# Two-layer GATv2 on one core: projection ahead of the scores, relus ahead of the weights, one set of waits a step

## What is computed

```python
xl = (x @ Wl + bl).reshape(n, HEADS, DIM)
xr = (x @ Wr + br).reshape(n, HEADS, DIM)
e = jax.nn.leaky_relu(xl[src] + xr[dst], NEG_SLOPE)
score = jnp.einsum('ehd,hd->eh', e, att)
smax = jax.ops.segment_max(score, dst, num_segments=n)
ex = jnp.exp(score - smax[dst])
denom = jax.ops.segment_sum(ex, dst, num_segments=n)
alpha = ex / (denom[dst] + 1e-16)
out = jax.ops.segment_sum(xl[src] * alpha[..., None], dst, num_segments=n)
```

## Time and profile before

| | us |
|---|---|
| median of 3 runs | 2266.37 |
| span of the profiled execution | 2743.9 |
| PE busy in it | 1964.3 (72%) |
| POOL busy | 1543.5 (56%) |
| ACT busy | 1411.6 (51%) |
| DVE busy | 1302.8 (47%) |
| DMA engines, mean over the span | 121 GB/s |

### The profile page before, as it was taken

One profiled execution on the slowest core, in us unless ns is written; L12 is line 12 of the kernel. 1 busy time (PEld: TensorE's weight loads), 2 busy tenths in 40 slices (PEclk: granted clock), 3 DMA queues, 4 the chain that ended last, 5 costly groups with the idle time before them and its releaser, 6 DMA issues. The chain is left out here.

```text
span 2743.9 us, 66371 instructions
## 1 busy us (share of the span) xinstructions
PE 1964.3 (72%) x19001; PEld 1307.1 (48%) x19001; DVE 1302.8 (47%) x5318; ACT 1411.6 (51%) x3474; POOL 1543.5 (56%) x1664
## 2 busy tenths in 40 slices
PE   4567777777777777777744777777777777777775
PEld 2234555554554555545533445544545545555453
DVE  7324554554544544544541344444444444444445
ACT  4324555555555555555542455555555555555554
POOL 4656666565566566565315666566556565565540
PEclk9778988989999998998966898999998999889997
DMA  5544444444454454444214444444444444444430
GB/s 133 166 111 127 127 130 128 132 130 128 130 131 128 129 132 129 128 133 128 73 56 117 122 125 128 126 121 129 128 125 128 123 125 127 125 124 128 124 107 7
DMA packets 236750, 332.67 MB, mean 121 GB/s; under 512 B 51011, under 2 KB 160491, under 8 KB 236395
## 3 DMA queue, kind: packets, MB, share of 16 engines
q0 software_dynamic: 75072, 208.30, 29.4%
q1 hardware_dynamic: 161322, 120.16, 14.9%
HBM read 308.02 MB, written 20.25 MB: 120 GB/s over the span
## 5 line engine op out<-in xcount | busy, mean ns | idle before, releaser
L982 POOL DMA_INDIRECT rows<-table,src_t x1564 | 1492.5, 954 | 995.5 <-PE psum L1182 367.9
L1428 DVE SCALAR_TENSOR_TENSOR acc<-acc,keep,psum 128x129 f32 x782 | 273.2, 349 | 1164.2 <-PE psum L1182 596.9
L1207 ACT COPY wgt<-psum 128x256 f32<-128x256 f32 x392 | 146.0, 373 | 1030.2 <-PE psum L1190 649.4
L1089 PE MATMUL psum<-lz,att_w 128*32 128x256 f32 x3128 | 281.2, 434 | 513.6 <-ACT lz L1200 444.6
L1103 PE MATMUL psum<-ident,rows 128*128 128x128 f32 x3128 | 578.4, 315 | 34.9 <-DMA rows<-table,src_t 34.9
L1103 PEld LDWEIGHTS psum<-ident,rows 128*128 128x128 f32 x3128 | 412.3, 160 | 237.5 <-issue 187.8
L1200 ACT ACTIVATE lz<-psum 128x512 f32<-128x512 f32 x782 | 427.8, 603 | 41.0 <-DMA table<-row 14.4
L1182 PE MATMUL psum<-rows,wgt 128*32 128x129 f32 x6256 | 313.8, 302 | 49.3 <-issue 45.9
L1089 PEld LDWEIGHTS psum<-lz,att_w 128*32 128x32 f32 x3128 | 64.4, 113 | 590.0 <-ACT lz L1200 509.4
L1106 PE MATMUL psum<-oh,xrw 96*128 96x256 bf16 x1564 | 344.4, 306 | 0.0
L1279 ACT ACTIVATE ex<-hold_s,peak 128x256 f32<-128x256 f32 x392 | 201.5, 514 | 138.4 <-issue 87.4
(11 more groups left out here) (257 smaller groups left out, 2100.1 us busy)
## 6 DMA issues: line engine op xcount, KB each, us to landing
xrw<-xr_split SPq DMA_DIRECT2D x782, 48.0 KB
relb<-rel_d SPq DMA_DIRECT2D x194, 192.0 KB
rows<-table,src_t POOLq DMA_INDIRECT x1564
relb<-cyc_d SPq DMA_DIRECT2D x194, 64.0 KB
xr_split<-split SPq DMA_DIRECT2D x50, 192.0 KB, 1.9
table<-row SPq DMA_DIRECT2D x50, 130.0 KB, 2.1
x_mid<-x SPq DMA_DIRECT2D x25, 64.0 KB
xo<-x_mid SPq DMA_DIRECT2D x25, 64.0 KB
```

The lines of the kernel that those rows point to most:

```text
L982: pool.indirect_dma_start(rows[:, ring(u), t, u % M, :, :].rearrange("p h c -> p (h c)"), None, s["tables"][layer][0:NP, :], bass.Indirect ...
L1089: m = pe.matmul(out[o:o + W, 0:UE], w["att_w"][:, h * W:h * W + W], lz[:, u % M, h * UE:h * UE + UE], start=False, stop=True, skip_group_c ...
L1428: m = v.scalar_tensor_tensor(a, a, s["keep"][:, u:u + 1], sum_bank(i - 6)[:, c:c + D + 1], ALU.mult, ALU.add)
```

## The change

- **PE order.** A step begins with the transposes of exp of step i-4, which stood at its end. Then come node stages 5, 13 and 9, then `project(i)` for both units, then `score(i-1)`, then the sums of step i-5 and the node work. Within the node work the combining matmuls (L1143) go from the end to the front.
- **PE waits.** `project` takes a whole step. Rows are counted by one semaphore for each of ten ring places, ranges by one for each of four. It waits once for rows and bank ahead of the first transpose, and once for range and one-hots ahead of the first one-hot matmul.
- **Masks.** The mask matmul of a unit, 64 columns wide, becomes two of 32 columns.
- **ACT order.** The relus of step i (before: of step i-1) come after the first node work, then the weights of step i-4 (before: i-5), the other node work, exp of step i-3 (before: i-4), then the scores of step i-1 (before: i-2), then `lin` of step i, which no longer waits for rows itself.
- **Buffers.** `lz`, the relus' output, gets four places, not two.
- **DVE.** `lowest` takes step i-2, not i-3, in the same place.

The diff, without the moved blocks that are the same on both sides:

```diff
-    rows_in = [sem(f"rows_in{i}") for i in range(ROWS)]
-    xr_in = [sem(f"xr_in{i}") for i in range(4 * M)]
+    rows_in = [sem(f"rows_in{i}") for i in range(ROWS // M)]
+    xr_in = [sem(f"xr_in{i}") for i in range(4)]
...
-    lz = sb("lz", [P, M, H * UE], F32)
+    lz = sb("lz", [P, 2 * M, H * UE], F32)
...
+    def rows_of(i):
+
+        return 16 * K * sum(len(of_step(j)) for j in range(i % (ROWS // M), i + 1, ROWS // M))
+
+    def xr_of(i):
+
+        return 16 * sum(len(of_step(j)) for j in range(i % 4, i + 1, 4))
...
                 for u in of_step(g):
-                    at = u % M * HW
-                    pe.matmul(out[at:at + HW, 0:UE], s["mask_w"][:, :], oh[:, u % (3 * M), :],
-                              start=False, stop=False, skip_group_check=True)
+                    for h in range(H):
+                        o = u % M * HW + h * W
+                        pe.matmul(out[o:o + W, 0:UE], s["mask_w"][:, h * W:h * W + W], oh[:, u % (3 * M), :],
+                                  start=False, stop=False, skip_group_check=True)
...
-            def project(u):
-
-                z = ps[u % M]
-                pe.wait_ge(rows_in[u % ROWS], (u // ROWS + 1) * (16 * K))
-                pe.wait_ge(xr_in[place(u)], (u // (4 * M) + 1) * 16)
-                pe.wait_ge(oh_ready, u // M + 1)
-                hold(pe, lz_ready, u - M + 1)
...
+            def project(i):
+
+                pe.wait_ge(rows_in[i % (ROWS // M)], rows_of(i))
+                hold(pe, lz_ready, i * M)
+                for u in of_step(i):
+                    z = ps[u % M]
...
+                    if u == of_step(i)[0]:
+                        pe.wait_ge(xr_in[i % 4], xr_of(i))
+                        pe.wait_ge(oh_ready, i + 1)
...
             for i in range(END):
+                if of_step(i - 4):
+                    pe.wait_ge(ex_ready, i - 3)
+                    hold(pe, wgt_ready, i - 4)
...
+                    m.then_inc(ex_turned, 1)
...
+                if of_step(i):
+                    project(i)
                 if of_step(i - 1):
                     score(i - 1)
-                for u in of_step(i):
-                    project(u)
...
                 node_work(i)
-                if of_step(i - 4):
-                    pe.wait_ge(ex_ready, i - 3)
-                    hold(pe, wgt_ready, i - 4)
...
             def relu(u):
 
                 act.wait_ge(z_ready, u + 1)
-                hold(act, score_ready, u // M)
...
+                hold(act, score_ready, u // M - 1)
...
             for i in range(END):
-                new = of_step(i - 1)
-                if of_step(i - 5):
-                    act.wait_ge(ex_turned, i - 4)
-                    hold(act, sums_ready, i - 6)
...
-                for u in new:
-                    relu(u)
...
+                for u in of_step(i):
+                    relu(u)
+                if of_step(i - 4):
+                    act.wait_ge(ex_turned, i - 3)
+                    hold(act, sums_ready, i - 5)
...
+                old = of_step(i - 3)
...
+                    act.wait_ge(max_ready, min(i - 1, NO))
+                    hold(act, ex_turned, i - 4)
...
+                new = of_step(i - 1)
...
+                    act.wait_ge(score_ready, i)
+                    hold(act, ex_ready, i - 4)
...
                 new = of_step(i)
                 if new:
-                    for u in new:
-                        act.wait_ge(rows_in[u % ROWS], (u // ROWS + 1) * (16 * K))
...
-                if of_step(i - 3):
-                    lowest(i - 3)
+                if of_step(i - 2):
+                    lowest(i - 2)
```

More of the change, by code:

```diff
@@ L1054, in _ @@
             sp.sem_inc(listed)
-            for k in range(4 * M):
-                sp.wait_ge(xr_in[k], 16 * len(range(k, NU, 4 * M)))
+            for k in range(4):
+                sp.wait_ge(xr_in[k], xr_of(max(range(k, NO, 4))))
             for c in range(RING // RELS):
@@ L1089, in score @@
                         m = pe.matmul(out[o:o + W, 0:UE], w["att_w"][:, h * W:h * W + W],
-                                      lz[:, u % M, h * UE:h * UE + UE], start=False, stop=True, skip_group_check=True)
+                                      lz[:, u % (2 * M), h * UE:h * UE + UE], start=False, stop=True, skip_group_check=True)
                 m.then_inc(score_ready, 1)
-            def project(u):
-                z = ps[u % M]
-                pe.wait_ge(rows_in[u % ROWS], (u // ROWS + 1) * (16 * K))
-                pe.wait_ge(xr_in[place(u)], (u // (4 * M) + 1) * 16)
-                pe.wait_ge(oh_ready, u // M + 1)
-                hold(pe, lz_ready, u - M + 1)
[L1100 to L1108, removed]
@@ new lines, in node_work @@
+            def node_work(i):
+                for q, tl in [(0, nodes(i, -1)), (1, nodes(i, 0))]:
+                    for t in tl:
+                        pe.wait_ge(staged, t + 1)
+                        if t < NT - 1:
+                            hold(pe, z2_ready if last else xrf_ready, t - 1)
+                        else:
+                            pe.wait_ge(lz_ready, NU)
+                        for m in range(2):
+                            for c in range(3):
+                                mm = pe.matmul(bank(t)[m * HW:m * HW + HW, q * (D + 1):q * (D + 1) + D + 1],
+                                               s["sel"][:, c, :, :].rearrange("p h w -> p (h w)"),
+                                               stg[t % 2][:, 2 * (2 * q + m) + c, :], start=(c == 0),
+                                               stop=(c == 2), skip_group_check=True)
+                        if q == 1:
+                            mm.then_inc(comb_ready, 1)
@@ L1133, in node_work @@
                                   ).then_inc(next_proj, 1)
[L1134 to L1148, removed]
-            for i in range(END):
+            for i in range(END):
+                if of_step(i - 4):
+                    pe.wait_ge(ex_ready, i - 3)
+                    hold(pe, wgt_ready, i - 4)
+                    for t in range(K):
+                        m = pe.transpose(ps[4][:, t * P:t * P + P], ex[:, (i - 4) % 2, t * P:t * P + P],
+                                         s["ident"][:, :])
+                    m.then_inc(ex_turned, 1)
                 for t in nodes(i, 5):
```

44 lines of the change are left out of this document (22 added, 22 removed).

## The result

The changed kernel takes 2211.86 us (median of 4 runs, 2206.33 to 2213.86); the kernel before took 2266.58 us beside it (4 runs, 2265.63 to 2268.64). The ratio is 0.9756, with a 95% interval of 0.974 to 0.9773. So 55 us are gained where the prediction forecast 79, and the time lies 25 us above the forecast and inside its range. The profiled execution of after took 2206.33 us, with a span of 2204.6.

What follows compares the result with a forecast made beforehand. The prediction took a loop of PE and ACT, 5.22 us a step unprofiled, to bound the kernel, with the gathers' 5.02 next. Its sum was 219.7 + 2 × 983.7 = 2187 us, range 2130 to 2271.

Steps and rivals of the forecast that it cites:

- What bounded the kernel before: PE and ACT pass in turns through a loop of 4.88 us plus node work; the gathers' 5.02 us lies close.
- The profile's own cost: In the edge steps, profiling delays semaphores by 1.22 us a step, so savings are priced against 5.22 us, not 6.44.
- Relus off the path: Ahead of PE's attention matmuls the 1.11 us wait goes; at most 1.13 us a step, at least nothing.
- The new loop and PE's work: Exp, transposes, projection, relus and weights take about 4.5 us a step on PE and ACT; PE's own work 4.6.
- The gathers' pace as the new bound: POOL's four gathers a step, 1.254 us each, 5.02 us in all, become the bound and PE follows.
- The sum: Whole kernel: 219.7 us outside the edge steps plus 983.7 for each of two passes, 2187 us, 79 below the median.
- Waits and masks: On PE, fewer projection waits give 0 to 0.2 us a step, split mask matmuls 0.05; nothing below the gathers' pace.
- Gathers quicker without the profile: Rival on POOL: unprofiled gathers are faster, so PE's loop of 4.5 us sets the time, 1984 us; chance 0.09.
- ACT and PE by turns: Rival: ACT's whole work and PE's part add up to 5.7 us a step, 2454 us; chance 0.08.
- No change: Rival: the unprofiled kernel already runs at the gathers' pace and PE's wait is free, 2266 us; chance 0.07.
- Half of it: Rival for half the gain: node bursts, lower clock or late rows keep steps at 5.1 us, 2215 to 2261; chance 0.13.
- DVE starves the gathers: Rival: each pair of DVE's one-hots stops POOL, adding 0.59 us a step, 2418 us; chance 0.03.

Runs made afterwards that it cites:

- before_third: The kernel before, unchanged, profiled on a chip of the lower level: 2264.94 us, beside a median of 2265.72 us.
- after_unit_waits: The changed kernel with rows and ranges counted by unit again and four waits ahead of each unit's projection: 2207.74 us, ratio 0.9739.
- before_half_gathers: The kernel before with one gather a unit in place of two: 2257.67 us on the upper-level chip, 2239.04 us on a lower-level one.

## Why the prediction came out as it did

**What bounded the kernel before: right.** The loop through the transposes of exp, the weights, the relus and the attention matmuls set the time, as read from the earlier trace rows. Half of the gathers took 27 us from it and moving the relus took 56. The reading of the earlier trace rows, that POOL stood idle for over 600 us in waits for sums, holds for the upper level alone (there 514 us lie beyond the usual 0.30); at the lower one it is 23 us.

**The profile's own cost: wrong.** The step that called the 1.22 us a step between profile and median "the profile's own cost" failed, and with it the expectation of 2250 to 2450 us for the profile after, whose span is 2204.6. Spans and unprofiled times differ by under 3 us on either level: 2745.1 against 2747.55, 2263.3 against 2265.72. The conclusion drawn from it, to price the saving against 5.22 us and not 6.44, held, since 5.22 was worked out from the median; the reason given for it did not. That median and result both lie at the lower level, and only the profile at the upper, was luck: at the upper level no run of the changed kernel stands against the sum.

**Relus off the path: right.** PE's wait there fell from 332.0 us (343 waits of about 1 us in the clean trace) to nothing. The prediction said below 50.

**The new loop and PE's work: right in size, 4.55 measured against 4.5, with gathers halved; not right in every part.** The prediction put `lowest` beside the loop, with 2.14 us of DVE against 3.3 of PE and ACT, and at nothing. With half of the gathers the exp waits for it for 115.0 us in 152 steps. The 4.5 also holds a doubling of the table loads and 0.25 us for node stages that were estimates, and steps with and without node work differ widely: by phase of the eight steps that a tile takes, the distance from one exp to the next is 3.7 to 6.3 us on average in pass one. That the total came out within 0.05 us is in part luck. Right, too, was the reading that of the 0.62 to 0.72 us a step that PE could give only part is paid out: from 5.22 to 4.55 is 0.67 us, or 263 us; 55 of them came.

**The gathers' pace as the new bound: right.** With all gathers back the kernel pays 207 us for them. The signs are those that were named: PE waits for rows at L1111 (225.3 us in 157 steps, where `before_third` has 52.8 in 24), gathers start 1.25 us apart, POOL waits for sums 57 times and never beyond the usual 0.30 us. The last of these says less than it seems: the kernel before has 58 such waits at the lower level, 40.4 us in all. Half of the sign for the half-gain case is there as well: PE waits for exp in 128 steps (189.3 us), but beside a POOL that doesn't wait. In a kernel that is paced by something else, a wait between two engines that have time to spare is no sign of a loss.

**The sum: three terms too small, 2187 against 2211.9.** The largest is the time from the last gather to the last projection of a pass, put at 4.3 us; it measured 8.4 and 6.6. The ends of the two edge stretches in the trace of after, first gather, last gather and last projection of each pass:

```profile
92.82 1.18 POOL L990 DMA_INDIRECT rows<-table,src_t  x1 [3.96 <-issue]
1080.10 0.94 POOL L990 DMA_INDIRECT rows<-table,src_t  x1 [0.30 <-issue]
1088.16 0.38 PE L1117 MATMUL psum<-oh,xrw 96*128 96x256 bf16 x2
1155.43 0.97 POOL L990 DMA_INDIRECT rows<-table,src_t  x1 [3.73 <-POOLq L129]
2136.79 0.99 POOL L990 DMA_INDIRECT rows<-table,src_t  x1 [0.30 <-issue]
2143.02 0.38 PE L1117 MATMUL psum<-oh,xrw 96*128 96x256 bf16 x2
```

From the first gather to the last are 987.3 and 981.4 us, where 781 distances of 1.254 made 979.4: +7.9 and +2.0 (the mean distance is 1.264 and 1.257). From the last gather's start to the end of the last projection are 8.4 and 6.6, where 4.3 was put: +4.1 and +2.3. The pieces outside are 92.8 + 66.9 + 61.2 = 220.9 where 219.7 was put: +1.2. Together 17.5 us, and 2187.1 + 17.5 is the span, 2204.6. The last 7 us to the median are the 1.7 us by which this run exceeds its span, and the scatter of the runs, of which the profiled one was the fastest.

The pace and the end of a pass have different causes. The pace: in pass one a gather takes 0.959 us on average and the time between two is 0.305, where 0.954 and 0.30 were put, and 781 times 0.010 are the 7.9 us; in pass two it is 0.952 and 0.305, and 2.0 us. No gap in either pass is longer than 0.35 us, so POOL was never held up: the 57 waits for sums (17.4 us) are the usual 0.30 us under another name. The mean is carried by few: 92 of the 1564 gathers take more than 1.0 us, 14 us in all over the usual 0.95, 55 of them in pass one. Long gathers were in the kernel before too (135, 24 us, in `before_third`), so this isn't a cost of the change. They go with node work on DVE: its product in the gelu (L1546, 0.68 us long, 50 times in all) stands beside 23 of the 92 long gathers and beside 25 of the 1472 others, and the 48 gathers beside it take 1.09 us on average. This is a count; no run took that work away.

The end of a pass: the prediction counted only what the rows need to land and be projected. PE's last steps show what stands ahead of that (from the last gather of pass one on):

```profile
1081.84 0.44 PE L1167 MATMUL psum<-ident,ex 128*128 128x128 f32 x2 [0.66 <-ACT ex L1284]
1082.11 0.60 PE L1111 MATMUL psum<-ident,rows 128*128 128x128 f32 x4
1084.91 1.15 PE L1133 MATMUL psum<-stg,sel 128*64 128x129 f32 x12
1086.08 0.44 PE L1167 MATMUL psum<-ident,ex 128*128 128x128 f32 x2
1086.73 1.16 PE L1180 MATMUL psum<-w,ge 128*128 128x128 f32 x8 [0.21 <-DVE ge L1546]
1087.73 0.60 PE L1111 MATMUL psum<-ident,rows 128*128 128x128 f32 x4
```

By the 3.6 us of the prediction the last rows have landed at 1083.7. PE projects them at 1087.73, because it is in the step before (1082.11), and then has the combined sums (L1133), exp and a node stage (L1180) ahead of the next projection. The wait for the later of two units, which the prediction names as paid once in a pass, isn't it: the last step has one unit, and with waits for each unit (`after_unit_waits`) the lag is 1087.68 − 1079.16 = 8.5 us.

**Waits and masks: nothing at this pace, as said**, for the waits by `after_unit_waits`. The masks were not tried by themselves.

**The rivals.** *Gathers quicker without the profile* (1984 us) and *ACT and PE by turns* (2454) are excluded by the traces and the time. *No change* had something to it: in `before_third` POOL is hardly held up either, and its gathers start 1.296 and 1.266 us apart on average in the two passes. But the median distance of gathers is 1.25 us in every trace, and PE falls behind them, which is what the change could shorten. *Half of it* described an average step of 5.1 us, above the pace of 5.02, by bursts or late rows. The average edge step of after is (995.7 + 988.0) / 392 = 5.06 us, half way between, and the time, 2211.9, lies only 3 us from the 2215 at which that case began. The trace decides, not the number: the gathers keep the 1.254 us to 0.5%, and the rest is added at the ends of the passes. *DVE starves the gathers*: from `before_third` to after DVE's share of the span rose from 58% to 59% and the mean gather fell from 962 to 956 ns, so the price of 0.59 us a step isn't seen. In after the 308 gathers with over 0.3 us of a one-hot beside them take 0.961 us on average, the 1084 with none 0.951, and the median of both is 0.946. The rule of the Trainium skill, "SBUF — State Buffer", section "Summary: rules for kernel authors", can have at most the 14 us of long gathers here; whether these are its doing is open, and so is which mode DVE was in, which no trace here shows.

## What to carry to other kernels

An engine that works in program order should first do what has long been released and is waited for: here the relus stood behind a copy that itself had to wait for PE, and exchanging the two brought all that the whole change brought. Before pricing such a saving, find the next bound and its pace (four gathers of 1.254 us), since of 0.67 us a step that the loop gave up only 0.14 came out. Halving the work of the suspected bound tells in one run what it costs: 27 us before the change, 207 after it, both on one chip. And where a ring of buffers lies between two engines of nearly the same pace, look at how far the second is behind at the end, not at the first one's waits alone.

## What the runs showed of the hardware that was not expected

The same kernel takes 2747.55 us on one chip and 2262 to 2269 on three others, with the profile off, and the trace of the slow level reads as if semaphores came late: waits of DVE, POOL and ACT name "remote" (497.7 us for DVE's accumulations), a wait for relus lasts up to 11.0 us instead of 1.1. On SP's queue four range loads near 101 us take 11.37 us; at the lower level the same four, in `before_third`, take this:

```profile
100.74 4.00 SPq L1006 DMA_DIRECT2D xrw<-xr_split  x4
```

Of SP's MOVE and SEQ_ASSERT instructions, which take 18 to 38 ns at the lower level, 43 to 63 of each kind took over 0.5 us in the two upper traces of the kernel before, mostly some 0.7. Half of the gathers brought the kernel before to 2257.67 us on that chip, 0.83% above its 2239.04 elsewhere, but the changed one to 2080.5, 3.8% above its 2004.28. So of the 482 us between the levels of the kernel before only 19 are left when half of the gathers are left out, and fewer of the slow register instructions too (15 and 10 of the two kinds in `before_half_gathers`). The loss needs the full gathers, then, though a gather itself takes no longer there (954 ns against 962). What slows the kernel is open, and so is whether it belongs to the chip or passes; that the profile isn't the reason is shown.
